# Where the first of three maximum units stands in a turn of the last cross-attention

## Chip, cores and metric

The kernel runs on one core of one Trainium2 chip. The metric is the device time of one execution in microseconds (us); the three runs of the kernel before took 2480.80, 2481.84 and 2481.87 us, median 2481.84.

## What is computed

The reference is a model of four layers, each with a cross-attention over 12544 context rows of width 256, a mixer over 128 rows, and a feed-forward part. The change touches the cross-attention of layer 3 alone, with 16 heads of width 16 and a mask for each query and key:

```python
sim = jnp.einsum('bhqd,bhkd->bhqk', q, k) / jnp.sqrt(jnp.asarray(dh, q.dtype))
bias = NEG_BIAS * (~mask).astype(sim.dtype)
weights = jax.nn.softmax(sim + bias[:, None, :, :], axis=-1)
out = jnp.einsum('bhqk,bhkd->bhqd', weights, v)
```

Here q has 128 rows, k and v have 12544.

## The kernel before

`Heads16.run` does this attention for layer 1 (tiles named l1x, masks by key, table `UNITS_BY_KEY`) and for layer 3 (tiles named l3x, masks by query and key, table `UNITS_BY_PAIR`). The keys are cut into 14 chunks of 896, each of 7 tiles of 128 keys. For a chunk the kernel does two things that lie in different bodies of the loop:

- **Maxima.** 16 maximum units, numbered 0 to 15 (u0 to u15 below), one for each head. A unit is two matmuls of 448 columns by `max_unit` (L1787) from the bf16 keys `high` into one of two PSUM buffers `pm`, by the unit's parity, and one VectorE operation by `maximum` (L1631) that reads the buffer and takes the running maximum. Unit x waits on TensorE until VectorE has read unit x-2 (L1783). The two matmuls of a unit use rows 32g and 32g+64 of the array (modulo 128), where g = (x mod 8) // 2.
- **Scores and weights.** 28 quads (four heads, one tile of 128 keys, into one of three banks `ring`), each four matmuls (L1807) and one for the mask (L1811); ScalarE takes the exponent of a quad (L1718). A pair is two quads. `weigh` adds a pair's 8 products with the values into `O` (L1854).

TensorE's order is written out by hand in `body`. One turn t of seven does four steps: the quads of pair 2t+2, the quads of pair 2t+3, the `weigh` of the pairs 2t and 2t+1, and maximum units in up to three places. Turn 6 begins the next chunk's quads. The table says in which place a unit stands: (t, 0) is between the two pairs of quads, (t, 1) is behind the second pair and ahead of the weights, and (t, 2) is behind the weights. The first list is for units 12 to 15 of the chunk one ahead (turns 0 and 1), the second for units 0 to 11 of the chunk two ahead (turns 2 to 6). So in the kernel before the turns 4 and 6 have three units, two ahead of the weights and one behind them; the turns 0, 1, 2, 3 and 5 have two.

VectorE's order in a turn is the units of the turn in the order of their numbers, whatever their places, and around them: in turn 0 first the rescaling of `O` (L1670, which waits for all weights of the chunk before) and the copy of the mask; in turn 2 first the gap of the maxima and a mask row; in turn 3, behind u2 and u3, `split_top` (L1648 and L1650: three casts and two subtractions, each waiting for the one before). The first `weigh` of turn 0 waits for the rescaling. In turn 3 TensorE also turns the maxima (L1794) and spreads the factors (L1798).

SyncE stores the split maxima and loads them into `q_rows` (L1573, L1576); the first quad of turn 6 needs them. It loads the next keys once the first pair of a chunk has been weighed and `high` once a chunk's maxima have been read. GpSimd copies the values once a chunk has been weighed.

Of the kernel before, what the change touches and what calls it, by code (L numbers as in the profile page):

```python
# [987 lines left out]
def attend(nc, S, R, heads, per_chunk, q, chunks, w_v, bias_v, top, masks, O, sums, last_tile=None, side=None):  # L988
# [317 lines left out]
UNITS_BY_KEY = (12, ((0, 0), (0, 0), (1, 0), (1, 0)), (  # L1306
    (2, 0), (2, 0), (3, 0), (3, 0), (4, 0), (4, 0), (4, 2), (5, 0), (5, 0), (6, 0), (6, 0), (6, 2)))
UNITS_BY_PAIR = (12, ((0, 1), (0, 1), (1, 1), (1, 1)), (
    (2, 1), (2, 1), (3, 1), (3, 1), (4, 1), (4, 1), (4, 2), (5, 1), (5, 1), (6, 1), (6, 1), (6, 2)))
GAP_TILE, TOP_PAIR, SPLIT_TILE, FACTOR_PAIR = 2, 8, 3, 9  # L1310
PROBS = 8

# [2463 lines left out]
```

## Time and profile before

| | us |
|---|---|
| median of three runs | 2481.84 |
| the profiled execution, its own time | 2482.87 |
| its span, first to last instruction | 2481.1 |
| TensorE busy | 2228.8 |
| VectorE busy | 1826.3 |
| ScalarE busy | 1185.9 |
| GpSimd busy | 519.5 |

The execution took 1.77 us more than its span. The loop of the last cross-attention lies between about 2043 and 2397 us of the span. A difference of the span is a difference of the time.

### The profile page before, as it was taken

What the parts mean: (1) busy time and instruction counts of PE and PEld (TensorE: products, weight loads), DVE (VectorE), ACT (ScalarE), POOL (GpSimd) and SP (SyncE); (2) the same over time, 40 slices, a digit from 0 to 9 for tenths busy, and PEclk for the clock granted to TensorE, in tenths of its full rate; (3) what the DMA queues carried; (4) which work ended last, traced back from release to release, by engine and by line L of the source; (5) the groups of instructions that cost most, each with busy time, mean ns of one, the idle gap of its engine ahead of it and who ended that gap; (6) DMA issues with size and microseconds to landing.
All of it is one profiled execution on the core that took longest, in us unless ns stands there. A gap on an engine that the chain in (4) does not pass through costs nothing. (4 is left out here: it accounts for less than half of the span.)

```text
span 2481.1 us, 56935 instructions
## 1 busy us (share of the span) xinstructions
PE 2228.8 (90%) x21794; PEld 1434.9 (58%) x21794; DVE 1826.3 (74%) x2833; ACT 1185.9 (48%) x2053; POOL 519.5 (21%) x300
## 2 busy tenths in 40 slices
PE   2999979999996969999988899999997559999979
PEld 1444436666665836666667555566655415555548
DVE  6788878999996267777734688888886877777721
ACT  4566653344444337888763333323232416565542
POOL 0555540000000030000001166655552010000000
PEclk7999999999997969999998999999998759999989
DMA  8577765676655567878745322222211347677654
GB/s 285 204 243 242 237 222 142 193 208 188 175 176 196 190 151 186 183 181 184 177 105 193 122 104 71 85 104 104 104 60 51 106 110 172 158 167 165 154 149 171
DMA packets 245977, 398.00 MB, mean 160 GB/s; under 512 B 28921, under 2 KB 210304, under 8 KB 245668
## 3 DMA queue, kind: packets, MB, share of 16 engines
q1 hardware_dynamic: 240132, 393.90, 55.4%
q8 instruction: 143, 2.34, 0.4%
q10 hardware_dynamic: 5664, 1.44, 0.3%
q14 instruction: 38, 0.31, 0.0%
HBM read 316.44 MB, written 78.06 MB: 159 GB/s over the span
## 5 line engine op out<-in xcount | busy, mean ns | idle before, releaser
L1631 DVE CUSTOM_DVE_ANT_0 l3x_junk<-l3x_pm,l3x_mrow,l3x_top 128x896 bf16<-128x896 f32 x224 | 247.0, 1148 | 73.3 <-PE l3x_pm L1787 68.3
L1715 ACT ACTIVATE l1x_prob<-l1x_ring,mask_col 128x512 f32<-128x512 f32 x392 | 248.2, 685 | 81.5 <-PE l1x_ring L1807 80.0
L1718 ACT ACTIVATE l3x_prob<-l3x_ring 128x512 f32<-128x512 f32 x392 | 204.6, 601 | 154.1 <-PE l3x_ring L1811 152.8
L2800 POOL TENSOR_TENSOR l2x_gk<-l2x_f,first_vin 128x1024 f32<-128x1024 f32 x98 | 184.3, 1917 | 161.1 <-DVEq L2541 161.1
L1174 ACT ACTIVATE l0x_att_pt<-l0x_att_pt 128x1024 f32<-128x1024 f32 x99 | 104.7, 1058 | 167.4 <-DVE l0x_att_pt L1115 163.9
L1207 PE MATMUL l0x_att_pv<-l0x_wv,l0x_att_vin 128*128 128x512 f32 x392 | 181.9, 607 | 0.0
L2674 PE MATMUL l2x_kf<-l2w_w,l2x_nin 128*128 128x512 f32 x392 | 173.4, 602 | 4.5 <-DVE l2x_f L2515 4.5
L2674 PE MATMUL l2x_kf<-l2w_w,l2w_first 128*128 128x512 f32 x392 | 170.2, 594 | 0.0
L2515 DVE SCALAR_TENSOR_TENSOR l2x_f<-l2x_kf,l2x_rs,l2w_bias 128x1024 f32<-128x1024 f32 x98 | 125.8, 1284 | 55.6 <-PE l2x_kf L2674 42.7
L1631 DVE CUSTOM_DVE_ANT_0 l1x_junk<-l1x_pm,l1x_mrow,l1x_top 128x896 bf16<-128x896 f32 x112 | 123.6, 1148 | 43.8 <-PE l1x_pm L1787 43.8
L1811 PE MATMUL l3x_ring<-l3x_ident,l3x_mtile 128*128 128x512 bf16 x392 | 151.4, 386 | 0.0
L1631 DVE CUSTOM_DVE_ANT_0 l1x_junk<-l1x_pm,first_mrow,l1x_top 128x896 bf16<-128x896 f32 x112 | 123.5, 1148 | 36.3 <-PE l1x_pm L1787 36.2
L2717 PE MATMUL l2x_M<-l2x_gk,l2x_f 128*64 128x130 f32 x1568 | 134.3, 275 | 0.0
L2674 PEld LDWEIGHTS l2x_kf<-l2w_w,l2x_nin 128*128 128x128 f32 x392 | 74.8, 193 | 98.3 <-issue 89.7
L2674 PEld LDWEIGHTS l2x_kf<-l2w_w,l2w_first 128*128 128x128 f32 x392 | 73.9, 190 | 90.8 <-issue 88.4
L1122 DVE TENSOR_TENSOR l0x_sums<-l0x_sums,l0x_att_pt 128x1024 f32<-128x1024 f32 x99 | 120.9, 1221 | 6.6 <-ACT l0x_att_pt L1174 1.1
L2519 DVE TENSOR_REDUCE first_vin<-l2x_f 128x8 f32<-128x1024 f32 x98 | 119.6, 1220 | 3.4
L1115 DVE TENSOR_TENSOR l0x_att_pt<-l0x_att_ps,l0x_att_tops 128x1024 f32<-128x1024 f32 x99 | 116.5, 1217 | 5.5 <-PE l0x_att_ps L1224 5.3
L2629 ACT ACTIVATE l2x_fsq<-l2x_f 128x1024 f32<-128x1024 f32 x49 | 51.8, 1058 | 138.3 <-DVE l2x_f L2515 138.3
L2629 ACT ACTIVATE first_vin<-l2x_f 128x1024 f32<-128x1024 f32 x49 | 51.8, 1057 | 134.7 <-DVE l2x_f L2515 134.7
L1207 PEld LDWEIGHTS l0x_att_pv<-l0x_wv,l0x_att_vin 128*128 128x128 f32 x392 | 70.7, 190 | 76.6 <-issue 70.8
L2722 PE MATMUL l2x_M<-l2x_gk,l2x_f 128*64 128x66 f32 x1568 | 112.3, 221 | 0.0
(737 smaller groups left out, 4950.6 us busy)
## 6 DMA issues: line engine op xcount, KB each, us to landing
first_kt<-scratch_KS SPq DMA_DIRECT2D x84, 448.0 KB, 9.1
scratch_KT<-l0x_max_kf SPq DMA_DIRECT2D x28, 896.0 KB, 4.7
l0x_att_kt<-scratch_KT SPq DMA_DIRECT2D x56, 448.0 KB, 7.1
scratch_KS<-l0x_side_kp SPq DMA_DIRECT2D x14, 1344.0 KB, 13.4
l1x_kt<-scratch_KS SPq DMA_DIRECT2D x42, 448.0 KB, 9.4
scratch_KS<-first_kt SPq DMA_DIRECT2D x14, 1344.0 KB, 5.9
l3x_kt<-scratch_KS SPq DMA_DIRECT2D x42, 448.0 KB, 8.9
l0fw_w<-L_ffn_exp_w SPq DMA_DIRECT2D x16, 1024.0 KB, 7.8
```

The lines of the kernel that those rows point to most:

```text
L1115: dve.tensor_tensor(pt[at][:, :, :], psc[u][:, :, :].rearrange("p a (b q) -> p (a b) q", q=P), tops[:, :, :], ALU.subtract).then_inc(sem(f ...
L1122: dve.tensor_tensor(sums[:, :, :], sums[:, :, :], pt[buffer(i, t)][:, :, :], ALU.add).then_inc(sem(f"summed{u}"), 1)
L1207: last = pe.matmul(pv[vb][:, 0:heads * vd], vin[b][:, d, s * P:(s + 1) * P], w_v[:, d, :], start=(d == 0), stop=(d == DC - 1))
L1631: dve.tensor_tensor_reduce(junk[x % 2][:, :, :], pm[x % 2][:, :, 0:SPLIT], mrow[b][:, :].rearrange("p (s k) -> p s k", s=2), 1.0, top[1 - ...
L1715: ins = act.activation(into, scores, ACT.Exp, bias=R.mask_col[:, bass.ds(m * TILES + n // 4, 1)])
L1718: ins = act.activation(into, scores, ACT.Exp)
L1811: last = pe.matmul(bank[:, :].rearrange("p (k q) -> p k q", q=P), self.mtile[b][:, t * P:(t + 1) * P], R.ident16[:, :].unsqueeze(1).broadc ...
L2515: dve.scalar_tensor_tensor(f[b][:, t, :], pf[u][:, :, :].rearrange("p a n -> p (a n)"), rs[:, at:at + 1], bias[:, :], ALU.mult, ALU.add).t ...
L2519: dve.tensor_reduce(ks[b][:, 0, t, :], f[b][:, t, :].rearrange("p (h d) -> p h d", h=H), AX.X, ALU.add).then_inc(S.counted(f"sums{b}"), 1)
L2674: last = pe.matmul(pf[u][:, n, :], nin[b][:, c, t * P:(t + 1) * P], w[:, c, n * BANK:(n + 1) * BANK], start=(c == 0), stop=(c == DC - 1))
L2717: last = pe.matmul(pM[64 * g:64 * g + 64, pair // 2, upper(pair)], f[b][:, t, h * HD:h * HD + HALF], gk[b][:, t, h, :], start=False, stop= ...
L2800: pool.tensor_tensor(gk[b][:, t, :, 0:HD], f[b][:, t, :].rearrange("p (h d) -> p h d", h=H), ks[b][:, 2, t, :].unsqueeze(2).broadcast_to([ ...
```

## The change

```diff
 UNITS_BY_PAIR = (12, ((0, 1), (0, 1), (1, 1), (1, 1)), (
-    (2, 1), (2, 1), (3, 1), (3, 1), (4, 1), (4, 1), (4, 2), (5, 1), (5, 1), (6, 1), (6, 1), (6, 2)))
+    (2, 1), (2, 1), (3, 1), (3, 1), (4, 0), (4, 1), (4, 1), (5, 1), (5, 1), (6, 0), (6, 1), (6, 1)))
```

In turn 4 the units u4, u5, u6 move from "two ahead of the weights, one behind" to "one between the pairs of quads, two ahead of the weights, none behind". In turn 6 the same is done with u9, u10, u11. The number of each unit's turn stays, so VectorE's instructions and their order are the same; only TensorE's order differs. The chunks 12 and 13 have no chunk two ahead, so the two turns come 12 times each. Layer 1 has its own table and is not touched.

## Rows read from the trace of the kernel before

**Rows 1.** Stretches: us, busy us of PE, PEld, DVE, ACT, POOL, then PEclk, DMA share, GB/s.

```profile
2027.71:2031.24 3.53, 3.53 (x22) 2.19 (x21) 1.61 (x4) 1.79 (x3) 0.00 (x0) 0.50 0.71 225
2132.22:2158.52 26.30, 24.78 (x406) 15.60 (x402) 20.43 (x42) 15.70 (x31) 1.68 (x1) 1.00 0.72 161
2370.00:2377.00 7.00, 4.79 (x80) 3.22 (x82) 0.00 (x0) 3.50 (x7) 0.00 (x0) 1.00 0.15 26
```

**Rows 2.** PE: weights of the turns 0 and 1 that follow.

```profile
2146.54 1.07 PE L1854 MATMUL l3x_O<-l3x_prob,l3x_v 128*17 128x128 f32 x32
2147.54 0.40 PE L1807 MATMUL l3x_ring<-l3x_q_rows,first_kt 99*128 99x128 bf16 x4
...
2149.90 1.07 PE L1854 MATMUL l3x_O<-l3x_prob,l3x_v 128*17 128x128 f32 x32
```

**Rows 3.** Longest waits of PE, window 2054:2353: us in total, times, longest us.

```profile
PE l3x_pm L1787 <- DVE l3x_top L1631: 13.3, 24, 0.7
```

**Rows 4.** PE instructions of a turn 4: start us, us, instruction [idle before <-releaser].

```profile
2132.22 0.40 PE L1807 MATMUL l3x_ring<-l3x_q_rows,l3x_kt 99*128 99x128 bf16 x4
...
2132.90 0.38 PE L1811 MATMUL l3x_ring<-l3x_ident,l3x_mtile 128*128 128x512 bf16 x1
2133.12 0.39 PE L1807 MATMUL l3x_ring<-l3x_q_rows,l3x_kt 99*128 99x128 bf16 x4
...
2133.78 0.38 PE L1811 MATMUL l3x_ring<-l3x_ident,l3x_mtile 128*128 128x512 bf16 x1
2134.10 0.36 PE L1787 MATMUL l3x_pm<-l3x_high,l3x_qb 32*128 32x448 bf16 x1
...
2134.58 1.09 PE L1854 MATMUL l3x_O<-l3x_prob,l3x_v 128*17 128x128 f32 x32
2136.37 0.36 PE L1787 MATMUL l3x_pm<-l3x_high,l3x_qb 32*128 32x448 bf16 x1 [0.70 <-DVE l3x_top L1631]
...
2136.67 0.40 PE L1807 MATMUL l3x_ring<-l3x_q_rows,l3x_kt 99*128 99x128 bf16 x4
```

**Rows 5.** PE instructions of a turn 6, with the weights before it.

```profile
2138.84 1.07 PE L1854 MATMUL l3x_O<-l3x_prob,l3x_v 128*17 128x128 f32 x32
2140.06 0.38 PE L1807 MATMUL l3x_ring<-l3x_q_rows,first_kt 99*128 99x128 bf16 x4 [0.15 <-issue]
...
2141.93 0.36 PE L1787 MATMUL l3x_pm<-l3x_high,l3x_qb 32*128 32x448 bf16 x1
...
2142.22 1.07 PE L1854 MATMUL l3x_O<-l3x_prob,l3x_v 128*17 128x128 f32 x32
2143.70 0.36 PE L1787 MATMUL l3x_pm<-l3x_high,l3x_qb 32*128 32x448 bf16 x1 [0.41 <-DVE l3x_top L1631]
...
2143.99 0.40 PE L1807 MATMUL l3x_ring<-l3x_q_rows,first_kt 99*128 99x128 bf16 x4
```

**Rows 6.** DVE: the first unit of that turn 6, and the rescaling behind it.

```profile
2142.48 1.15 DVE L1631 CUSTOM_DVE_ANT_0 l3x_junk<-l3x_pm,l3x_mrow,l3x_top 128x896 bf16<-128x896 f32 x1 [1.15 <-PE l3x_pm L1787]
...
2145.70 0.70 DVE L1670 TENSOR_TENSOR l3x_O<-l3x_O,l3x_F 128x512 f32<-128x512 f32 x1
...
2146.60 1.15 DVE L1631 CUSTOM_DVE_ANT_0 l3x_junk<-l3x_pm,l3x_mrow,l3x_top 128x896 bf16<-128x896 f32 x1
```

**Rows 7.** DVE instructions of the turn 4 of rows 4.

```profile
2132.37 1.15 DVE L1631 CUSTOM_DVE_ANT_0 l3x_junk<-l3x_pm,l3x_mrow,l3x_top 128x896 bf16<-128x896 f32 x1
...
2133.44 0.21 DVE L1648 CAST l3x_top_parts<-l3x_topT 16x128 bf16<-16x128 f32 x1
...
2134.57 0.21 DVE L1648 CAST l3x_top_parts<-l3x_topT 16x128 bf16<-16x128 f32 x1
2135.16 1.15 DVE L1631 CUSTOM_DVE_ANT_0 l3x_junk<-l3x_pm,l3x_mrow,l3x_top 128x896 bf16<-128x896 f32 x1 [0.38 <-DVE l3x_top_parts L1648]
...
2136.23 1.15 DVE L1631 CUSTOM_DVE_ANT_0 l3x_junk<-l3x_pm,l3x_mrow,l3x_top 128x896 bf16<-128x896 f32 x1
```

**Rows 8.** PE: an idle time of over 2 us in the same loop.

```profile
2374.77 0.38 PE L1807 MATMUL l3x_ring<-l3x_q_rows,l3x_kt 99*128 99x128 bf16 x4 [2.21 <-issue]
```

## The prediction

> **What bounds the kernel now.** I read the stretches first, for one chunk of the loop [rows 1]. In 26.30 us TensorE is busy for 24.78, VectorE for 20.43, ScalarE for 15.70. VectorE has some 6 us to spare in a chunk, so it doesn't bound the loop by its sum; TensorE is the thread on which everything hangs, and it loses time only where it waits. A turn is the unit to count in. A turn of two units with no wait takes 3.36 us: 2.36 to its weights, and 1.00 from their start to the next quad [rows 2]. Then I read where TensorE waits. Between 2054 and 2353 us it waited 24 times, 13.3 us in all, for VectorE to read a maximum buffer [rows 3]; that is twice per chunk, in the turns 4 and 6, at the third unit. In a turn 4 the wait is 0.70 us [rows 4], in a turn 6 it is 0.41 us [rows 5]. That is what the change could win at most, 12 x 1.11 = 13.3 us.
>
> Next, what each of the two waits hangs on. A third unit x+2 may start once VectorE has read unit x. In turn 6 VectorE is idle when u9 comes: u9's matmul starts at 2141.93, its read at 2142.48, and u11's matmul at 2143.70 [rows 5, 6]. So with an idle VectorE it is 1.77 us from a unit to the unit after next. In turn 4 it is longer, 2134.10 to 2136.37, 2.27 us [rows 4], and the timeline of VectorE says why: it is not idle when u4 arrives. It reads u3 from 2132.37 to 2133.44, works through the chain of `split_top` until 2134.57 + 0.21, and starts u4's read at 2135.16, though u4's matmul had started at 2134.10. The read ends where u5's begins, at 2136.23, and u6 goes 0.14 us later [rows 4, 7]. This is the row that decides the case: **the third unit of turn 4 is released at 2136.37 by a chain u3, split, u4 on VectorE, which starts before the turn does and doesn't contain u4's place on TensorE.**
>
> **The change, part by part.** No instruction is added or removed, no DMA is issued elsewhere, and VectorE's order stays. Only TensorE's order in two of seven turns differs, 12 times each.
>
> *Turn 4, u4 earlier.* A unit between two pairs of quads: from the last mask to a unit is 0.32 us (2133.78 to 2134.10), from a unit to a quad 0.30 (2136.37 to 2136.67), in place of 0.22 from mask to quad (2132.90 to 2133.12) [rows 4]. The insertion costs 0.32 + 0.30 - 0.22 = 0.40 us. u4 would start at 2132.90 + 0.32 = 2133.22, 0.88 earlier. Its buffer is free, as u2 has been read by 2132.37. The gain is nothing: VectorE can't read it before 2135.16 anyway [rows 7].
>
> *Turn 4, u6 ahead of the weights.* The second quads are done by 2133.78 + 0.40, so u5 starts at about 2134.50. u6 must wait for u4's read, as before until 2136.37. This wait of about 1.9 us now stands ahead of the weights, which are ready to go, and TensorE's queue is in order. In the kernel before, the weights (1.00 us and more) covered most of it and 0.70 was left. Now the weights begin at 2136.37 + 0.29 and the next turn at 2136.37 + 0.29 + 1.00 = 2137.66, where it was 2136.67: **+0.99 us**. The insertion cost doesn't add to that, since it lies within the wait. The cover for the wait that goes is the weights themselves, so the whole 1.00 appears. Bounds: 0.90, if the weights' first loads are already in when u6 goes; 1.10, if the weights start as late behind one unit as behind two in series (2134.10 to 2134.58, 0.48 against 0.29). I take 0.99, from the nearest rows [rows 4, 5].
>
> *Turn 6.* Here VectorE is idle when u9 comes, so an earlier u9 does help. Seen from the turn's start: u9 at 0.68 + 0.32 = 1.00, u11 at 1.00 + 1.77 = 2.77, the weights at 3.06, the next turn at 4.06. It was 3.93 (2140.06 to 2143.99) [rows 5]. **+0.13 us.** What is gained by the early start (1.87 to 1.00, 0.87) is less than what is lost by having no weights in front of u11 (1.00). Without any wait, u10 would go at 1.88 + 0.40 = 2.28, u11 at 2.48, as the two share rows of the array, and the turn would take 3.76: -0.17. Upper end 0.40, if the ring of three banks or the exponents make the second quads later. I take 0.13. u9 needs u7's read; after the later turn 5 VectorE reads u7 and u8 well before the end of u9's matmul, as it does now.
>
> *Turn 0.* Now its weights start 2.55 us into the turn (2143.99 to 2146.54), 0.19 later than the free 2.36, as they wait for the rescaling, which VectorE starts at 2145.70, behind u9, u10 and u11 [rows 2, 5, 6]. After the change the three are read from 1.56 to about 4.98 into turn 6 (u10 is ready at 2.28 + 0.56, so 2.84, and two reads of 1.07 follow), the rescaling starts at 4.98, and its weights may go 0.84 later, at 5.82, as they do now. They come at 4.06 + 2.36 = 6.42. The wait is gone: **-0.19 us**; between -0.19 and 0.
>
> *Turn 5 to 6.* The step from the weights of turn 5 to the first quad of turn 6 took 1.22 us in this chunk in place of 1.00 [rows 5], since the split maxima came late through SyncE into `q_rows`; three of the twelve do, this one by most. The split isn't moved and turn 6 begins 0.99 later, so this is hidden: about -0.5 us in all.
>
> *Other queues.* SyncE's loads wait for turns 0 and 1, which keep their distances. Weights that end later in turn 4 hold back ScalarE only for the exponents of turn 5, which need the buffers of pair 8 and come behind those weights on TensorE in any case. The copy of the values on GpSimd waits for turn 6's weights, a period ahead of its use.
>
> The sum: 12 x (0.99 + 0.13 - 0.19) - 0.5 = 12 x 0.93 - 0.5 = **+10.7 us**. The span goes from 2481.1 to 2491.8. The profiled execution took 2482.87, 1.03 over the median; the difference carries over to the median: 2481.84 + 10.7 = 2492.5 us, +0.43%. All ends together would give 12 x (0.90 - 0.17 - 0.19) - 0.5 = +6.0 and 12 x (1.10 + 0.40) = +18.0.
>
> **The rivals.**
> *Faster: the early unit frees the third.* If VectorE read u4 as soon as it came, u6 would go at 1.00 + 1.77 = 2.77 into turn 4, as u11 in turn 6, and the turn would take 4.06 for 4.45, -0.39. With turn 6 and turn 0 that is 12 x (-0.39 + 0.13 - 0.19) = -5.4, 2476.4 us. It speaks for it that the first unit does come 0.88 earlier and that turn 4's wait is the longer of the two. It speaks against it that the read of u4 starts at 2135.16 for another reason, 0.38 behind the last cast [rows 7]. It decides at the point where turn 4 costs +0.06, u6 then at 2132.22 + 3.22 and u4's read, 1.07 + 0.14 before it, at 2134.2: earlier than that the change is a gain, and the row stands 0.9 behind it. The Trainium skill (Perfetto Trace Analysis, Optimization Strategy) advises to find a gap, what releases it, and to make that dependency start sooner; read with the two waits alone it promises this rival, and the row above shows that the dependency on TensorE isn't the one that releases.
>
> *Smaller loss: turn 6 loses its wait.* If u11 needn't wait (VectorE a little quicker behind a lone unit), turn 6 gives -0.17 and the sum is 12 x (0.99 - 0.17 - 0.19) - 0.5 = +7.1, 2488.9 us. Against it: 1.77 us is a fixed sum of a read of 1.07 and the two handovers.
>
> *No change: the loss is given back.* TensorE would have to find 0.93 us of other waits in each chunk. Before the change there are only 0.41 and 0.19 in the turns 6 and 0, both in the sum. 2481.8 us, hardly likely.
>
> *Larger loss: the clock.* The new idle time ahead of u6, some 1.6 us, might lower TensorE's clock. At a granted clock of 0.50, the 1.2 GHz level, the four quads of a turn and the step to the units took 3.53 us [rows 1] against 1.88 at 1.00 [rows 4]; behind each of 12 waits that is 12 x 1.65 = 19.8 more, 2512 us. Against it: an idle time of 2.21 us in the same loop [rows 8] left the clock at 1.00, the 2.4 GHz level, in its stretch [rows 1]. The Trainium skill (TensorE: Matmul & The Clock Gate, What's actually happening) says that the throttled state is the default and activity releases it, which speaks against any new gap; by the row the gap is too small to matter.
>
> **How the numbers follow.** The forecast 0.84; the smaller loss 0.05; the clock 0.03; a larger loss in the quads or the weights, beyond 2496.5, 0.03; no change 0.02; faster 0.03. A measurement can tell 0.2%, 5.0 us, from no change. Faster by more than that: 0.03. Within it: 0.02, and 0.02 of the forecast and the smaller loss, 0.04. Slower: 0.93. The range runs from just below the smaller loss, 2488.5, to 2496.5, which covers turn 4 at 1.10 and turn 6 at 0.35.
>
> **What would show it.** In the profile after: u4 about 1.00 us into turn 4, yet VectorE's read of u4 as far behind `split_top` as before (0.38); TensorE's wait at u6 1.5 to 1.9 us; turn 4 of 5.44 us, turn 6 of 4.06, turn 0 of 3.36; a chunk of about 27.0 us; waits on VectorE of about 12 x 1.5 and 12 x 0.13 us. Idle time in front of the weights of turn 4 is the sign. If the read of u4 starts near 2.0 us into the turn in place of 2.94, the forecast is wrong and the faster rival holds.

## The result, and the profile after

The changed kernel took 2496.85 us (median of four runs, 2494.86 to 2498.36), the kernel before 2481.86 (2480.80 to 2482.03): the medians differ by 15.0 us. The ratio of the runs is 1.0054, 95% interval 1.0042 to 1.0066, which makes +13.4 us (10.4 to 16.4). Two further comparisons of the same two kernels, on other occasions, gave 1.0044 (1.0031 to 1.0057) and 1.0060 (1.0047 to 1.0073), +10.9 and +14.9 us. Below, "by the ratio" means such a product of a ratio and the median of the kernel before. One execution of a later kernel, the first of third_behind, took 3314.72 us at a mean granted clock of 0.642 and is left out of its ratio.

Turn 4 of the changed kernel, TensorE (start us, us, engine, line, instruction, idle before it and its releaser); it answers to [rows 4]:

```profile
2137.47 0.40 PE L1807 MATMUL l3x_ring<-l3x_q_rows,l3x_kt 99*128 99x128 bf16 x4
...
2138.14 0.38 PE L1811 MATMUL l3x_ring<-l3x_ident,l3x_mtile 128*128 128x512 bf16 x1
2138.46 0.36 PE L1787 MATMUL l3x_pm<-l3x_high,l3x_qb 32*128 32x448 bf16 x1
...
2138.75 0.40 PE L1807 MATMUL l3x_ring<-l3x_q_rows,l3x_kt 99*128 99x128 bf16 x4
...
2139.74 0.36 PE L1787 MATMUL l3x_pm<-l3x_high,l3x_qb 32*128 32x448 bf16 x1
...
2141.62 0.36 PE L1787 MATMUL l3x_pm<-l3x_high,l3x_qb 32*128 32x448 bf16 x1 [1.52 <-DVE l3x_top L1631]
...
2141.91 1.07 PE L1854 MATMUL l3x_O<-l3x_prob,l3x_v 128*17 128x128 f32 x32
2142.91 0.40 PE L1807 MATMUL l3x_ring<-l3x_q_rows,l3x_kt 99*128 99x128 bf16 x4
```

VectorE in the same turn; it answers to [rows 7]:

```profile
2138.69 0.21 DVE L1648 CAST l3x_top_parts<-l3x_topT 16x128 bf16<-16x128 f32 x1
...
2139.81 0.21 DVE L1648 CAST l3x_top_parts<-l3x_topT 16x128 bf16<-16x128 f32 x1
2140.41 1.15 DVE L1631 CUSTOM_DVE_ANT_0 l3x_junk<-l3x_pm,l3x_mrow,l3x_top 128x896 bf16<-128x896 f32 x1 [0.38 <-DVE l3x_top_parts L1648]
```

u4 stands 0.99 us into the turn in place of 1.88, and VectorE begins to read it at 2140.41, 2.94 into the turn and 0.38 behind the last cast, exactly as before. u6 goes at 4.15, exactly as before. What is new is that the weights come behind it. The turn takes 5.44 us.

Turn 6 and turn 0, TensorE; they answer to [rows 5] and the first of [rows 2]:

```profile
2146.09 0.40 PE L1807 MATMUL l3x_ring<-l3x_q_rows,first_kt 99*128 99x128 bf16 x4
...
2147.08 0.36 PE L1787 MATMUL l3x_pm<-l3x_high,l3x_qb 32*128 32x448 bf16 x1
...
2148.86 0.36 PE L1787 MATMUL l3x_pm<-l3x_high,l3x_qb 32*128 32x448 bf16 x1
...
2149.15 1.07 PE L1854 MATMUL l3x_O<-l3x_prob,l3x_v 128*17 128x128 f32 x32
2150.15 0.40 PE L1807 MATMUL l3x_ring<-l3x_q_rows,first_kt 99*128 99x128 bf16 x4
...
2152.51 1.07 PE L1854 MATMUL l3x_O<-l3x_prob,l3x_v 128*17 128x128 f32 x32
```

From u9 to u11 it is 1.78 us, turn 6 takes 4.06, and turn 0's weights come 2.36 into their turn, with no wait for the rescaling. TensorE's waits in the loop (us in total, times, longest), for [rows 3], and the stretches (columns as in [rows 1]):

```profile
PE l3x_pm L1787 <- DVE l3x_top L1631: 17.4, 12, 1.5
```

```profile
2137.47:2164.48 27.01, 25.23 (x405) 15.66 (x402) 20.60 (x42) 15.91 (x31) 1.84 (x1) 1.00 0.70 158
2222.60:2225.00 2.40, 2.33 (x35) 1.29 (x35) 2.15 (x6) 0.00 (x0) 0.00 (x0) 0.50 0.02 5
```

The first stretch is one chunk, 27.01 us for 26.30; the 26.30 hold the longest turn 5 of the kernel before, 0.22 us over the others. The second is what the forecast of the turns didn't have: behind one of the twelve waits, of 1.52 us, the granted clock is 0.50, the 1.2 GHz level, for over two microseconds. The instructions there:

```profile
2222.67 0.55 PE L1787 MATMUL l3x_pm<-first_high,l3x_qb 32*128 32x448 bf16 x1 [1.52 <-DVE l3x_top L1631]
2222.67 0.55 PE L1787 MATMUL l3x_pm<-first_high,l3x_qb_turned 32*128 32x448 bf16 x1
2223.15 1.91 PE L1854 MATMUL l3x_O<-l3x_prob,l3x_v 128*17 128x128 f32 x32
2224.99 0.61 PE L1807 MATMUL l3x_ring<-l3x_q_rows,first_kt 99*128 99x128 bf16 x4
```

The unit takes 0.55 us for 0.36, the weights 1.91 for 1.07. This turn 4 takes 6.48 us and the turn 5 behind it 3.64 for 3.18, together 1.50 over the others.

One table holds for all that follows. I took the turns from the timelines of TensorE (first quad to first quad), median of the twelve; "falls" counts the turns 4 with a granted clock of 0.50 in or right behind them; the loop runs from the second turn to the last transposes (L1897), with its irregular last chunk, which is called the tail below. The last column is the ratio to the kernel before. The turns and the loop of third_behind are those of its second profile, third_behind_look.

| kernel | turn 4 | turn 6 | turn 0 | falls | loop us | ratio (95%) |
|---|---|---|---|---|---|---|
| before | 4.44 | 3.94 | 3.55 | 0 | 353.9 | 1 |
| changed, the three profiles | 5.44 | 4.06 | 3.36 | 1, 3, 3 | 366.0, 369.7, 371.0 | 1.0054, 1.0044, 1.0060 |
| turn4_only | 5.44 | 3.94 | 3.55 | 2 | 370.4 | 1.0044 (1.0031 to 1.0057) |
| turn6_only | 4.45 | 4.06 | 3.36 | 0 | 353.0 | 1.0001 (0.9992 to 1.0010) |
| third_behind | 4.45 | 3.86 | 3.36 | 0 | 350.4 | 0.9984 (0.9975 to 0.9992) |
| split_first_after | 4.05 | 4.05 | 3.36 | 0 | 350.6 | 0.9971 (0.9961 to 0.9981) |
| split_first_before | 3.94 | 3.94 | 3.55 | 0 | 349.9 | 0.9981 (0.9971 to 0.9991) |
| split_first_spread | 3.86 | 3.86 | 3.36 | 0 | 344.8 | 0.9967 (0.9954 to 0.9980) |
| idle_filled | 5.44 | 4.06 | 3.36 | 0 | 364.2 | 1.0035 (1.0023 to 1.0046) |
| keys_earlier | 4.45 | 3.94 | 3.55 | 0 | 356.2 | 1.0019 (1.0010 to 1.0028) |
| spread_keys_earlier | 3.86 | 3.86 | 3.36 | 0 | 343.6 | 0.9948 (0.9935 to 0.9961) |

The profile of the changed kernel (span 2496.6 us, 15.5 over that of the kernel before) splits so: the loop is 12.1 us longer, of which 10.7 are the turns and 1.5 the one fall; 2.4 us lie ahead of the loop and 1.0 behind it, where both kernels have the same code.

The table doesn't count falls in the tail. There TensorE is idle once for over 2 us at the place of [rows 8] in five of the profiles: 2.21 (before), 2.59 (after_again), 2.33 (the third profile of the changed kernel), 2.20 (split_first_after) and 2.22 (split_first_before). Behind the last three the granted clock fell to 0.50. In split_first_before, whose listing has two lines more than that of the kernel before, so that L1809 and L1856 are its quads and weights:

```profile
2368.03 0.38 PE L1809 MATMUL l3x_ring<-l3x_q_rows,l3x_kt 99*128 99x128 bf16 x4 [2.22 <-issue]
...
2370.34 1.91 PE L1856 MATMUL l3x_O<-l3x_prob,l3x_v 128*17 128x128 f32 x32
```

### The profile page after: what moved, and what is told of

Its sections match the earlier page's. It is cut to its first block and busy times, and to the rows that moved or that the text cites. A ratio compares the mean times of both kernels' runs of the same rounds, so it can differ in the third digit from the quotient of the medians.

```text
span 2496.6 us, 56933 instructions
## 1 busy us (share of the span) xinstructions
PE 2237.1 (90%) x21792; PEld 1440.5 (58%) x21794; DVE 1831.9 (73%) x2833; ACT 1187.9 (48%) x2053; POOL 518.4 (21%) x300
## 6 DMA issues: line engine op xcount, KB each, us to landing
scratch_KS<-l0x_side_kp SPq DMA_DIRECT2D x14, 1344.0 KB, 13.4
```

## The experiments

Theory A: the third unit of turn 4 is released by a chain on VectorE (u3, split, u4) that its earlier start on TensorE can't touch, and the change puts the weights behind that wait.

### The two turns apart

```diff
 after_again: the changed table
 turn4_only:  (4, 0), (4, 1), (4, 1) ... (6, 1), (6, 1), (6, 2)
 turn6_only:  (4, 1), (4, 1), (4, 2) ... (6, 0), (6, 1), (6, 1)
```

> The changed kernel once more, to see what of its +15.0 us belongs to the loop and what to the rest. Theory A (the third unit stands ahead of the weights while VectorE still has the split in front of u4): turn 4 5.44 us, turn 6 4.06, turn 0 3.36, a chunk of 27.0 us and the loop 10 to 11 us longer than before; whatever is over that shows as single stalls at other places, in other chunks than in the first profile, and in stages that the change doesn't touch. Theory B (the change costs 15 us in its own turns): the turns of the loop sum to 14 to 15 us more than before.

> Only turn 4 has the new places, (4,0), (4,1), (4,1); turn 6 is as before. Theory A: turn 4 5.44 us, turn 6 3.94, turn 0 3.55; 12 x 0.99 - 0.5 = +11.4 us, a little slower than or equal to both together. Rival (each of the two turns costs alike, as each has a unit between its quads): about half of the whole, +5 to +7 us.

> Only turn 6 has the new places, (6,0), (6,1), (6,1); turn 4 is as before. Theory A: VectorE is idle when u9 comes, so u11 goes at 2.77 us into the turn; turn 4 4.45 us, turn 6 4.06, turn 0 3.36; 12 x (0.13 - 0.19) = -0.7 us, no change that can be told. Rival (each turn costs alike): +5 to +7 us.

Measured against the 2483.15 us of the kernel before on this occasion: the changed kernel 2494.80, turn 4 alone 2495.68, turn 6 alone 2482.68. By the ratios, turn 4 alone costs 10.9 us, all that the two cost together (10.9), and turn 6 alone 0.2 with an interval of -2.0 to +2.5. The rival by which each turn costs alike falls. The loop of turn4_only, 16.5 us over that of the kernel before, holds more than its turns 4 and two falls: 2.2 us stand in stalls of six turns 1, whose cause is told under keys_earlier. Of my split of the excess in after_again, one half held: stalls at other places in other chunks. The other half didn't: they stand in the turns 4, at the same wait, three falls of the clock, and the loop was 15.8 us longer, not 10 to 11. The chance of such a fall belongs to the change.

### The third unit back behind the weights

```diff
-(4, 0), (4, 1), (4, 1) ... (6, 0), (6, 1), (6, 1)
+(4, 0), (4, 1), (4, 2) ... (6, 0), (6, 1), (6, 2)
```

> The first unit of the turns 4 and 6 stands between the pairs of quads, as in the change, the second ahead of the weights and the third behind them, as before: (4,0), (4,1), (4,2) and (6,0), (6,1), (6,2). Theory A (the cost is the third unit's wait ahead of the weights; a unit between the quads is swallowed by the wait): u6 at 4.15 us into turn 4 and turn 4 4.45 as before; turn 6 2.28 + 0.29 + 1.00 + 0.29 = 3.86 us for 3.94 and turn 0 3.36 for 3.55; 12 x (-0.08 - 0.19) = -3.2 us. Rival (the cost is the unit between the quads): turn 4 stays near 5.4 us or gains at most 0.4, +5 us or more.

It took 2479.35 us (median of twelve runs) for 2483.15; the ratio gives -4.0 us (-6.2 to -2.0), with -3.2 forecast. The turns are those of a second profile.

> The kernel third_behind once more, for its profile. Theory A: turn 4 4.45 us with u6 at 4.15, turn 6 3.86, turn 0 3.36. Rival (the cost is the unit between the quads): turn 4 at 4.85 us or more.

That single run took 2474.29 us. Its turn 4, TensorE:

```profile
2151.34 0.40 PE L1807 MATMUL l3x_ring<-l3x_q_rows,first_kt 99*128 99x128 bf16 x4
...
2153.91 1.07 PE L1854 MATMUL l3x_O<-l3x_prob,l3x_v 128*17 128x128 f32 x32
2155.49 0.36 PE L1787 MATMUL l3x_pm<-first_high,l3x_qb 32*128 32x448 bf16 x1 [0.52 <-DVE l3x_top L1631]
...
2155.78 0.28 PE L1807 MATMUL l3x_ring<-l3x_q_rows,first_kt 99*128 99x128 bf16 x2
```

u6 at 4.15 again, and the turn at 4.44. The unit between the quads is still there and costs nothing, as the wait swallows it; the 0.70 of [rows 4] is 0.52 here, because the weights begin 0.2 later. So the microsecond is the place of the third unit, not that of the first.

### The split of the maxima ahead of u2 and u3

```diff
+ if t == SPLIT_TILE and exists(i, b, 1) and not keyed:
+     split_top(i1, b1, N * (m + 1) + full.index(("top", 0)) + 1)
  for unit in unit_list(i, b, t, 0) + unit_list(i, b, t, 1) + unit_list(i, b, t, 2):
      maximum(*unit)
- if t == SPLIT_TILE and exists(i, b, 1):
+ if t == SPLIT_TILE and exists(i, b, 1) and keyed:
```

> The changed table, and VectorE's split of the maxima in turn 3 ahead of u2 and u3 in place of behind them (for the query-key masks alone), where VectorE sat idle. Theory A (the chain u3, split, u4 on VectorE releases u6): u4 is read about 1.55 us into turn 4, u6 goes at 2.77 as u11 does, turn 4 is 4.06 us for 5.44; against the kernel before 12 x (-0.39 + 0.13 - 0.19) - 0.5 = -5.9 us. Rival (u6 ahead of the weights costs its microsecond whatever VectorE does first): turn 4 stays at about 5.0 to 5.4 us, +6 to +11 us.

> The kernel before with the split of turn 3 ahead of u2 and u3. Theory A: the third unit of turn 4, behind the weights, goes 1.77 us after u4 (3.65 into the turn) in place of 2.27; turn 4 3.94 us for 4.45, 12 x -0.51 - 0.5 = -6.6 us: as good as or a little better than the changed table with the same split. Rival (the order of the units matters more than the split): no more than -2 us.

> The split of turn 3 first, and the three units of the turns 4 and 6 one between the pairs of quads, one ahead of the weights, one behind them. Theory A: no third unit waits any more; turn 4 and turn 6 3.86 us each (2.28 + 0.29 + 1.00 + 0.29), turn 0 3.36; 12 x (-0.59 - 0.08 - 0.19) - 0.5 = -10.8 us against the kernel before. Rival (the waits come back elsewhere, on the exponents or the ring): -3 to -6 us.

Measured: split_first_after took 2476.30 us, split_first_before 2478.46, split_first_spread 2475.12; before 2482.93. By the ratios -7.2, -4.7 and -8.2 us. Turn 4 of split_first_after, TensorE (L1809, L1789 and L1856 are the quads, the units and the weights there):

```profile
2105.22 0.40 PE L1809 MATMUL l3x_ring<-l3x_q_rows,first_kt 99*128 99x128 bf16 x4
...
2106.21 0.36 PE L1789 MATMUL l3x_pm<-first_high,l3x_qb 32*128 32x448 bf16 x1
...
2107.99 0.36 PE L1789 MATMUL l3x_pm<-first_high,l3x_qb 32*128 32x448 bf16 x1
...
2108.28 1.07 PE L1856 MATMUL l3x_O<-l3x_prob,l3x_v 128*17 128x128 f32 x32
2109.28 0.40 PE L1809 MATMUL l3x_ring<-l3x_q_rows,first_kt 99*128 99x128 bf16 x4
```

u6 at 2.77 and the turn at 4.06: with the split out of the way the changed table does in turn 4 what the faster rival of the prediction promised (4.06), and the kernel is faster than before. That is the direct proof of the chain. All three have the turns 4, 6 and 0 that were expected, to 0.01 us in the median. Yet split_first_before and split_first_spread gained 1.9 and 2.6 us less than was forecast. Turn 5 shows a part of it: it was 3.18 us only in about half of the chunks and up to 3.87 in the rest, together 0.8 and 1.9 us over, where the forecast had nothing. SyncE's waits up to 2370 us, first before, then split_first_spread:

```profile
SPq L1576 <- DMA l3x_top_rows<-l3x_top_parts: 28.8, 12, 3.0
```

```profile
SPq L1576 <- DMA l3x_top_rows<-l3x_top_parts: 73.8, 13, 6.3
```

The store of the split maxima took 2.4 us a wait before and 5.7 here. It was issued 10.2 us behind the first of six key loads of 448 KB in place of 13.8, and in both kernels it landed 0.2 to 1.4 us behind the last of these loads, so that `q_rows` came hardly earlier. The kernel before holds the same case once: its thirteenth store, which lands behind the stretch of the first row, was issued 10.0 us behind the first key load and took 6.7 us. split_first_after gained more than its turns give (-7.2 by the ratio, -9.7 to -4.7), while its loop in the profile was only 3.3 us shorter. The profile is accounted for: the turns 4, 6 and 0 give -5.6, its turns 5 are 0.8 over those of the kernel before, and the fall in its tail costs some 1.5. What the other executions had over that stays open. My guess that split_first_before would be at least as good as it wasn't borne out; their intervals overlap.

### What the store waits for

```diff
-after(sp, weighed, PAIRS * m + begun)
+after(sp, weighed, PAIRS * m + begun - (0 if keyed else 1))
```

The line stands ahead of the load of the next stack of keys.

> The kernel before, with SyncE's load of the next chunk's stack of keys one turn earlier: once the last pair of the chunk before has been weighed, in place of the first pair of this one. It tells apart what the wait between turn 5 and turn 6 hangs on. If the store of the split maxima stands behind the key loads in the DMA engines: the three long turns 5 (0.06 to 0.22 us over 3.18) are gone and the tail is shorter, -0.5 to -2 us. Rival (the keys load no sooner, since the transfers are bound by the same traffic): no change.

> split_first_spread with the same earlier load. There the store of the split maxima, 2.2 us earlier, took 5.5 to 6.8 us to land in place of 2.3 to 3.5, so that turn 5 still waits (up to 0.69 us). If the key loads are in its way: store to load 2 to 3 us, turn 5 3.18 us throughout, 1.5 to 3 us under split_first_spread, some -10 us against the kernel before. Rival (another traffic is in its way): store to load still over 5 us and no gain.

keys_earlier took 2487.62 us for 2483.37, +4.7 by the ratio: slower, which neither theory had. Its store did land in 1.4 us in ten of thirteen cases, but the turns 1, 2 and 3 now hold stalls of up to 1.7 us in seven places. Four of them, 0.4 to 0.5 us each, are turns 1 in which u15 comes late because VectorE's copy of the mask took 1.50 to 1.64 us in place of 0.38. It had started while GpSimd copied the values (L1916). GpSimd and VectorE in the first of the four:

```profile
2066.32 1.68 POOL L1916 COPY l3x_v<-first_vin 128x1792 f32<-128x1792 f32 x1 [26.24 <-DMA first_vin<-ctx]
```

```profile
2066.61 1.64 DVE L1620 COPY l3x_mtile<-l3x_mrow 128x896 bf16<-128x896 bf16 x1
```

In the thirteen profiles that the table rests on, every copy of the mask that starts while this copy of GpSimd runs ends 0.24 to 0.25 us behind it (but for one that met its last 0.06 us); all others take 0.38 or 0.39. In its loop the kernel before has no such meeting, turn4_only has six. In the other three stalls the main wait has no releaser in the profile, and what they wait for stays open. The seven make some 4.6 us; the loop of this profile is only 2.3 us longer, mostly since the idle time of [rows 8] isn't there. spread_keys_earlier took 2468.11, -12.9 us (-10 expected). Its turn 5 is 3.17 or 3.18 throughout and its store lands as the first theory said:

```profile
SPq L1576 <- DMA l3x_top_rows<-l3x_top_parts: 32.0, 13, 3.5
```

So the key loads were in the way of the store. It has the lowest time here, 0.5% under the kernel before, though its interval and that of split_first_spread, measured on another occasion, still touch.

### The idle time filled

```diff
 for unit in unit_list(i, b, t, part):
+    if not keyed and t == 4 and part == 1 and unit[2] == 6:
+        for _ in range(6):
+            pe.matmul(O[:, :], zl[:, :], zr[:, :], start=False, stop=False, skip_group_check=True)
     max_unit(*unit)
```

> The changed kernel, and six matmuls of zeros of 512 columns into O (some 1.3 us) between u5 and u6 of turn 4, where TensorE waits 1.5 us; they add nothing to the result and hold u6 back by nothing. Theory A (in one to three of the twelve turns 4 the granted clock falls to 0.50 behind this wait, at 1.5 us each; that is the part of the loss over the forecast): turn 4 5.44 us every time, no stretch of the loop under a clock of 0.9, and a median 2 to 4 us under that of the changed kernel. Rival (the dips of the clock have nothing to do with the idle time): as many dips as in the changed kernel and the same time within 1 us.

> The changed kernel beside it on the same chip. Theory A: one to three turns 4 with a fall of the clock, each 6.4 us or so with a longer turn 5 behind it. Rival: none, and yet the same time.

On one chip: idle_filled 2492.72 us, the changed kernel 2498.72, before 2483.37. Turn 4 of idle_filled, and its clock over this turn and over the loop:

```profile
2111.84 1.47 PE L1890 MATMUL l3x_O<-l3x_zr,l3x_zl 128*128 128x512 bf16 x6
2113.43 0.36 PE L1787 MATMUL l3x_pm<-first_high,l3x_qb 32*128 32x448 bf16 x1
```

```profile
2110.00:2114.00 4.00, 3.89 (x38) 1.68 (x38) 3.48 (x10) 2.10 (x4) 0.00 (x0) 1.00 0.75 142
2044.00:2395.00 351.00, 344.95 (x5325) 210.84 (x5313) 255.27 (x505) 208.85 (x407) 20.47 (x12) 1.00 0.70 154
```

And the changed kernel beside it (after_third), one of its falls and the loop:

```profile
2109.50:2114.00 4.50, 4.37 (x53) 2.92 (x54) 2.21 (x6) 1.03 (x2) 0.00 (x0) 0.62 0.25 66
```

```profile
2044.00:2395.00 351.00, 327.25 (x5127) 203.56 (x5127) 252.83 (x498) 204.97 (x399) 20.44 (x12) 0.98 0.69 152
```

With six matmuls that do nothing, all inside the wait, the one profile has no fall in the loop, and the median is 6.0 us lower. The turns are unchanged at 5.44, and the loop is 10.3 us longer than before, where the forecast had 10.7; the ratio gives +8.7 (5.7 to 11.4). How strong is this? At 9 falls in 48 waits, twelve waits without one come by chance in about one profile of twelve (an estimate, 0.8125 to the twelfth power). The times carry more: of the five runs without the zeros one (2493.47) lies below the highest of the six with them (2494.32), and four lie above all six. The 6.0 us can't all be charged to the average of 2.25 falls, which is 3.5 us; on this occasion the changed kernel's profile had three falls in its turns 4 and one in the tail, which the zeros don't touch, some 6.2 us.

## Why the prediction was right, and where its size was off

- **The bound and the chain.** Right. The read of u4 didn't move, 2.94 us into the turn as before; turn6_only costs nothing, so the loss is in turn 4; and moving the split alone, under the changed table, takes u6 from 4.15 to 2.77.
- **The terms.** Turn 4 +0.99 (measured 5.44 for 4.45), turn 6 +0.13 (4.06 for 3.93 in that chunk, 3.94 in the median), turn 0 -0.19 (3.36 for 3.55), and no long turn 5 in the changed kernel except behind a fall. Each came out to 0.02 us, since each was a fixed distance read in the trace.
- **The cost of the unit between the quads** at nothing in turn 4: right, by third_behind.
- **The size.** +10.7 forecast, +15.0 measured between the medians, 0.35 us above the end of the range; by the ratios the three comparisons give 13.4, 10.9 and 14.9. That the range reached so near is luck: its upper end stood for a turn 4 at +1.10 and a turn 6 at +0.35, and neither came. The sum had no term for the clock, and the step that failed is the one that put it at nothing, the rival on the clock. It was set up as all or nothing, a fall behind each of the twelve waits for 19.8 us, and put aside because one idle time of 2.21 us had left the clock at 1.00 [rows 8]. In four profiles with this wait (three of the changed kernel, turn4_only) 9 of 48 turns 4 show a fall, at 1.5 to 1.6 us each where I had priced 1.65. That is 2.25 falls in a run and 3.5 us. With this term the forecast would have been 14.2. The profile of the first comparison itself had one fall, 1.5 us, and 3.4 us outside the loop, so the clock explains what the turns leave over in the loop, but not all that the forecast missed on that occasion. And the row that outvoted the rival was a lucky one: of five idle times of 2.2 to 2.6 us at its place, three had a fall behind them. One row where a thing didn't happen bounds how often it happens only loosely.
- **The Trainium skill** (TensorE: Matmul & The Clock Gate, What's actually happening) describes activity as what releases the throttle. The runs agree in kind: waits of 1.52 us brought falls in 9 of 48 cases, and the same twelve waits filled with matmuls of zeros brought none. I had let the row outvote it.
- **The spread.** The changed kernel's runs lay within 3.5 us of each other, those of before within 1.2 in the first comparison; one fall more or less, 1.5 us, may be a part of this, which runs without a profile can't show. The kernel before itself ran from 2477.58 to 2486.77 over 23 runs later, so other stages scatter too: the first instruction on a tile of layer 3 stood anywhere between 1983.3 and 1991.1 us in the profiles.

## What to carry to other kernels

When a unit is moved earlier on one engine, look at what its reader does at that time: if the reader is behind a chain of its own, nothing is gained, and only the places of the others have changed. Keep the instruction that has to wait behind work that is ready, never ahead of it; the wait is the same, but its cover is gone. Price idle time that a change adds on TensorE with a fall of the clock in some of the turns, not in all or none.

## What the runs showed of the hardware

- The granted clock fell to 0.50 behind 9 of the 48 waits at u6 (1.5 us in nearly all), and behind 3 of 5 idle times of 2.2 to 2.6 us in the tail of the same loop. It never fell behind the waits of 0.4 to 0.7 us, which stand behind the weights, in the profiles of the other kernels. Each fall lasted some 3 us and cost 1.5 to 1.6.
- Matmuls of zeros, 1.47 us in the row, put into the wait: no fall in twelve waits of one profile, and a median 6.0 us lower, though they do no work.
- A store of 12 KB landed in 1.4 us in most cases with no key load in flight (keys_earlier). With some in flight it landed 0.2 to 1.4 us behind the last of them: 2.3 to 3.4 us after its issue in the twelve regular chunks before, and 5.5 to 6.8 when it was issued 3.6 us sooner behind the six loads (split_first_spread).
- A VectorE copy of 128x896 bf16 from SBUF to SBUF takes 0.38 us, and up to 1.85 when it starts while GpSimd copies values: it then ends 0.25 us behind GpSimd's copy.
